# A recurrence on TensorE: part of the second output half's products moved ahead of the wait for the state's second half, its sums in banks by step, its input sums in nine pieces

## The chip, the core and the metric

One core of one Trainium2 chip. The metric is the device time of one execution in microseconds (us), the median of several runs. Engines are named PE (TensorE), ACT (ScalarE), DVE (VectorE), POOL (GpSimd) and SP (the queue that issues most DMAs).

## The reference, cut to what matters

The input x is 8 sequences of 512 steps with 256 features. It passes a recurrence, a long convolution, a gated scan and a mixture of 16 experts. The change is in the recurrence alone:

```python
xw = jnp.einsum('ntd,dh->nth', x, Wx) + b
def step(prev_h, xw_t):
    next_h = jnp.tanh(xw_t + prev_h @ Wh)
    return (next_h, next_h)
_, hs = jax.lax.scan(step, h0, jnp.swapaxes(xw, 0, 1))
```

There are 512 steps, each a product of an 8 x 256 state with a 256 x 256 matrix in float32 and a tanh, and each needs the one before.

## The kernel before

**Layout.** The state is kept transposed: 256 features in two halves of 128 partitions, `k` = 0 and 1 as input and `o` = 0 and 1 as output (h0 and h1 below), with 8 columns, one per sequence. `hring` holds the states of the last 16 steps; it is a part of the tile `tok`, and the trace names it so. PE's 128 columns are used as four tiles of 32 columns (`J` = 4, index `j`), so that one output half is four matmuls per input half. A matmul in float32 stands as two records in the trace, so the 16 matmuls of a step (2 output halves, 2 input halves, 4 tiles) are 32 records of line 531.

**One step** (`steps` on PE, line 523). PE waits for h0 of the step before (`s_h[0]`), multiplies it for o=0, waits for h1 (`s_h[1]`, line 529), multiplies it for o=0 and tells ACT (`s_sum[0]`, line 533). Then it does o=1 on both halves and tells ACT again (`s_sum[1]`). ACT (line 875) waits for each sum and writes tanh of it into `hring`, raising `s_h[0]` and `s_h[1]`.

**Input sums.** The sums of x with Wx and the bias are made eight steps at a time, a *group*, into PSUM, and the state products are added onto them. `inputs_summed(bank, n)` (line 502, matmuls on line 510) does one unit: n runs over the output half and, within it, the bias (`brow`, one row, with a row of ones) and the two halves of x (`xst`). That is six units of 4 matmuls, 64 columns (8 steps x 8 sequences) each. Group 0 of an iteration sums in PSUM banks 0 and 1 (o=0 and o=1), group 1 in banks 2 and 3; while one group's steps run, the other's input sums are made, one unit behind each of the steps t=1 to t=6.

**Filler.** `keep_up(256)` (line 489) is a matmul of zeros into an unused bank. It ends every step except the four (n=11 to 14 of 16) that carry two matmuls each of another part, `kernel_sums` (line 496), which makes the convolution's kernel.

**The other engines in the same loop** of 32 iterations of 16 steps: POOL copies each finished group of states away (line 426) and ACT waits for that once per group. ACT does one exponential for the convolution's kernel (line 879) in four steps. DVE takes the kernel sums out (line 1147), once per iteration. SP loads the x of each group (`ahead`, line 309) when PE has raised `s_xdone` at the group's last input unit; PE waits for the load (`s_xs`) at t=2. Everything behind the loop waits by semaphores for what it needs.

## Time and profile before

| | us |
|---|---|
| median of 3 runs | 1030.88 |
| lowest and highest run | 1028.31, 1051.01 |
| the profiled execution | 1021.49 |
| its span, first to last instruction | 1019.6 |
| PE busy, of the span | 967.6 |
| the recurrence's loop, about | 6.5 to 392 |

The numbers of a row come from the one profiled execution, so sums are made against 1021.49. PE's busy time counts a matmul from its start to its modelled end, and matmuls overlap. "PEld" is the loading of weights, which overlaps the matmuls as well. In a timeline, records of one line are merged into a row with its start, the time from the first start to the last end, and the number of records; `[0.37 <-PE ps L531]` says that the engine was idle for 0.37 us before and what ended it. The PEclk row gives the granted clock in tenths of 2.4 GHz.

### The profile page before, as it was taken

The page shows a single profiled execution, that of the slowest core. Times are in us where ns is not written, and L with a number is a line of the kernel's source. Part 1 is how long each engine was busy: PE and PEld are TensorE (multiplying, and loading weights), DVE is VectorE, ACT ScalarE, POOL GpSimd, SP SyncE. Part 2 cuts the span into 40 slices and gives each one's busy share as a digit, 9 for nine tenths or more (in the row PEclk, how much of TensorE's full clock was granted, in tenths as well). Part 3 has the DMA queues.
Part 4 walks back from the last instruction along what each step waited for, and adds up shares of the span by engine and source line. Part 5 has one row for each costly group of instructions (what it writes and reads, how often), then busy time and mean ns, then how long its engine had stood idle before and what let it go on. Part 6 is the DMA issues. An engine that isn't in the chain of part 4 may idle for free.

```text
span 1019.6 us, 58437 instructions
## 1 busy us (share of the span) xinstructions
PE 967.6 (95%) x25496; PEld 769.3 (75%) x25496; DVE 437.3 (43%) x932; ACT 574.5 (56%) x1956; POOL 309.5 (30%) x308
## 2 busy tenths in 40 slices
PE   8999999999999998779899999899999999999994
PEld 5777777777777777668544444688889999999994
DVE  1000000100000004558489979977556464656550
ACT  3555555555555557659487677623446565656551
POOL 3111111211111111324000346374024545454555
PEclk6999999999999999779899999999999999999998
DMA  3222222244554400875100111054066666566634
GB/s 91 83 93 86 94 100 83 83 78 55 56 60 56 55 11 11 171 141 102 45 0 1 42 42 70 11 207 155 21 204 133 152 130 155 126 155 124 138 43 51
DMA packets 85346, 89.59 MB, mean 88 GB/s; under 512 B 8657, under 2 KB 71654, under 8 KB 85298
## 3 DMA queue, kind: packets, MB, share of 16 engines
q1 hardware_dynamic: 69410, 71.50, 28.0%
q0 software_dynamic: 14592, 17.10, 10.1%
q8 instruction: 29, 0.48, 0.2%
q10 hardware_dynamic: 1296, 0.37, 0.2%
q14 instruction: 19, 0.16, 0.1%
HBM read 56.82 MB, written 33.96 MB: 89 GB/s over the span
## 4 chain that ended last, share of the span: by engine, by line
PE 80%; issue 5%; DVE 4%; POOL 4%; ACT 3%; DMA 3%; ACTq 0%; POOLq 0%; SPq 0%; DVEq 0%
PE ps L531 21%; PE ps L806 15%; PE ps L489 8%; PE ps L820 8%; PE ps L672 8%; PE ps L510 7%; PE ps L722 3%; POOL slots_in L452 2%; PE ps L594 2%; PE ps L579 2%; PE ps L496 2%; PE ps L731 2%; DMA slots_in<-tok,arena 1%; PE ps L582 1%; PE ps L749 1%
## 5 line engine op out<-in xcount | busy, mean ns | idle before, releaser
L875 ACT ACTIVATE tok<-ps 128x8 f32<-128x8 f32 x1024 | 172.8, 178 | 184.8 <-PE ps L531 184.2
L531 PE MATMUL ps<-tok,wh 128*32 128x8 f32 x16384 | 250.4, 181 | 2.3 <-ACT tok L875 2.1
L531 PEld LDWEIGHTS ps<-tok,wh 128*32 128x32 f32 x16384 | 203.4, 112 | 62.3 <-ACT tok L875 11.8
L1147 DVE TENSOR_SCALAR arena<-ps 128x127 f32<-128x127 f32 x32 | 9.3, 290 | 348.0 <-PE ps L496 348.0
L471 POOL DMA_INDIRECT out<-arena,dest x80 | 127.9, 1598 | 98.9 <-ACT arena L1033 79.7
L806 PE MATMUL ps<-xgT_hi,ew_hi 128*128 128x320 f32 (+1 forms) x384 | 118.8, 309 | 3.7 <-DVE spare L1288 1.6
L806 PE MATMUL ps<-xgT_hi,ew_lo 128*128 128x320 f32 (+1 forms) x384 | 119.0, 310 | 0.0
L806 PE MATMUL ps<-xgT_lo,ew_hi 128*128 128x320 f32 (+1 forms) x384 | 118.2, 308 | 0.0
L489 PE MATMUL ps<-zero 128*128 128x256 bf16 (+1 forms) x392 | 113.6, 293 | 1.3 <-POOL zero L399 1.3
L1394 DVE TENSOR_TENSOR mid<-mid,ps 128x320 f32<-128x320 f32 (+1 forms) x96 | 46.6, 486 | 106.0 <-issue 52.4
L672 PE MATMUL ps<-mid,gw 128*128 128x512 f32 x192 | 85.6, 604 | 2.4 <-ACT mid L961 1.6
L510 PE MATMUL ps<-xst,wx 128*32 128x64 f32 x2080 | 83.0, 227 | 0.0
L1051 ACT ACTIVATE mid<-ps 128x320 f32<-128x320 f32 (+1 forms) x96 | 41.9, 436 | 72.2 <-PE ps L806 68.8
L426 POOL TENSOR_TENSOR big<-tok,zero 128x128 f32 x64 | 28.9, 451 | 170.8 <-ACT tok L875 170.8
L452 POOL DMA_INDIRECT slots_in<-tok,arena x64 | 73.4, 1147 | 23.6 <-issue 17.1
L404 POOL TENSOR_TENSOR arena<-dta_q,iota_t 128x512 f32<-128x512 f32 x33 | 34.3, 1039 | 149.3 <-PE ps L496 148.2
L672 PEld LDWEIGHTS ps<-mid,gw 128*128 128x128 f32 x192 | 36.8, 194 | 47.7 <-issue 46.4
L806 PEld LDWEIGHTS ps<-xgT_hi,ew_hi 128*128 128x128 f32 (+1 forms) x384 | 68.7, 179 | 4.4 <-DVE spare L1288 1.9
L820 PE MATMUL ps<-ew_hi,eact_hi 128*128 128x256 f32 (+1 forms) x240 | 71.7, 299 | 0.3 <-ACT arena L1033 0.3
L806 PEld LDWEIGHTS ps<-xgT_lo,ew_hi 128*128 128x128 f32 (+1 forms) x384 | 68.8, 179 | 0.0
L806 PEld LDWEIGHTS ps<-xgT_hi,ew_lo 128*128 128x128 f32 (+1 forms) x384 | 68.6, 179 | 0.0
L820 PE MATMUL ps<-ew_hi,eact_lo 128*128 128x256 f32 (+1 forms) x240 | 67.8, 282 | 0.0
(206 smaller groups left out, 1782.5 us busy)
## 6 DMA issues: line engine op xcount, KB each, us to landing
ring<-k_pad SPq DMA_DIRECT2D x64, 256.0 KB, 6.3
slots_in<-mid SPq DMA_DIRECT2D x16, 645.0 KB, 3.5
mid<-slots_in SPq DMA_DIRECT2D x16, 645.0 KB, 4.2
arena<-in_ex_down SPq DMA_DIRECT2D x16, 384.0 KB
arena<-in_ex_gate SPq DMA_DIRECT2D x16, 352.0 KB
arena<-in_ex_up SPq DMA_DIRECT2D x16, 352.0 KB
xst<-in_x_steps SPq DMA_DIRECT2D x66, 64.0 KB, 1.8
xtok<-in_x_tok SPq DMA_DIRECT2D x16, 256.0 KB, 2.8
```

The costliest lines, as they stand in the source:

```text
L404: pool.tensor_tensor(kqx, d.unsqueeze(2).to_broadcast([P, KG * NH, P]), iota_t[:].unsqueeze(1).to_broadcast([P, KG * NH, P]), ALU.mult).th ...
L452: pool.indirect_dma_start(out=slots_in[:, :], out_offset=bass.IndirectOffsetOnAxis(ap=idx[:, k, r:r + 1], axis=0), in_=hid_tok[:, r, :], i ...
L471: pool.indirect_dma_start(out=out[:, :], out_offset=bass.IndirectOffsetOnAxis(ap=dest[:, z, t:t + 1], axis=0), in_=yo[:, z, t], in_offset= ...
L489: nc.tensor.matmul(ps[:, 6, 0:columns], zero16[:, 0:P], zero16[:, 0:columns], start=True, stop=True)
L510: last = nc.tensor.matmul(ps[Q * j:Q * j + Q, 2 * bank + o, 0:G * B], w, v, start=c < 0, stop=c == C - 1, skip_group_check=True, tile_posi ...
L531: last = nc.tensor.matmul(sums_at(bank, t, o)[Q * j:Q * j + Q], wh[:, k, columns(j, o)], hring[:, (n - 1) % (2 * G), k], start=False, stop ...
L672: last = nc.tensor.matmul(ps[:, gate_bank(n % NT, q), :], gw[:, q, c, z * P:(z + 1) * P], x1T[:, c, 4 * b:4 * b + 4, :].rearrange("p r t - ...
L806: last = nc.tensor.matmul(ps[0:fw, 2 * h + m % 2, 0:HALF], of(w)[:, c, f0:f0 + fw], v[:, c, hf * HALF:(hf + 1) * HALF], start=c == 0 and p ...
L820: last = nc.tensor.matmul(ps[:, 4 + (z + t) % 2, 0:D], a[0:fw, f, t * P:(t + 1) * P], down_of(w)[0:fw, f], start=f == 0 and p == 0, stop=f ...
L875: nc.scalar.activation(hring[:, n, o], sums_at(n // G, n % G, o), ACT.Tanh).then_inc(s_h[o], 1)
L1051: nc.scalar.activation(esil[0:fw, m % 2], ps[0:fw, m % 2, 0:HALF], ACT.Silu).then_inc(s_esil, 1)
L1394: nc.vector.tensor_tensor(eprod[0:fw, m % 2], esil[0:fw, m % 2], ps[0:fw, 2 + m % 2, 0:HALF], ALU.mult).then_inc(s_eact, 1)
```

## The change

Four things are changed, all in the recurrence.

1. In each step, the matmuls of the first two column tiles of o=1 on h0 are issued before the wait for h1. Those of the other two tiles come after o=0 is complete.
2. o=0's sums of a group stay in one bank (0 or 1), with even steps in its first half and odd ones in its second. o=1's sums go to a bank by the step's parity: banks 2 and 3 for group 0, 5 and 7 for group 1. The host orders each group's x in the same way (even steps, then odd).
3. The input sums are nine units: three of 64 columns for o=0, and three of 32 columns for each of the two banks of o=1. They stand behind the steps t=1 (two), t=2 (two), t=3, t=4, t=5 (one each) and t=6 (two).
4. `keep_up(256)` is called at t=0 and t=7 alone.

```diff
--- before.py
+++ after.py
@@ -260,7 +260,9 @@
         FIRST_LOADED, STATE_LOADED, LOADED, LATE = 16 * len(first), 16 * len(state), 16 * len(loads), 16 * len(late)
 
         NT = 2 * C
-        NIN = C * (C + 1)
+        LATER = (2, 3, 5, 7)
+        NIN = 3 * (C + 1)
+        INPUTS = {1: (0, 2), 2: (2, 4), 3: (4, 5), 4: (5, 6), 5: (6, 7), 6: (7, NIN)}
 
         def gate_bank(t, q):
             return (2 * t) % 6 + q if q < 2 else 2 + t
@@ -273,7 +275,10 @@
 
         def sums_at(bank, t, o):
 
-            return ps[:, 2 * bank + o, B * t:B * t + B]
+            if o == 0:
+                at = B * (G // 2 * (t % 2) + t // 2)
+                return ps[:, bank, at:at + B]
+            return ps[:, LATER[2 * bank + t % 2], B * (t // 2):B * (t // 2) + B]
 
         def columns(j, o):
 
@@ -501,16 +506,26 @@
 
             def inputs_summed(bank, n):
 
-                o, c = n // (C + 1), n % (C + 1) - 1
+                part, c = n // (C + 1), n % (C + 1) - 1
+                o, at = ((0, slice(0, G)), (1, slice(0, G // 2)), (1, slice(G // 2, G)))[part]
+                to = (bank, LATER[2 * bank], LATER[2 * bank + 1])[part]
+                cols = B * (at.stop - at.start)
                 for j in range(J):
                     if c < 0:
-                        w, v = brow[0:1, columns(j, o)], ones
+                        w, v = brow[0:1, columns(j, o)], ones[:, 0:cols]
                     else:
-                        w, v = wx[:, c, columns(j, o)], xst[:, bank, c].rearrange("p t b -> p (t b)")
-                    last = nc.tensor.matmul(ps[Q * j:Q * j + Q, 2 * bank + o, 0:G * B], w, v, start=c < 0, stop=c == C - 1,
+                        w, v = wx[:, c, columns(j, o)], xst[:, bank, c, at].rearrange("p t b -> p (t b)")
+                    last = nc.tensor.matmul(ps[Q * j:Q * j + Q, to, 0:cols], w, v, start=c < 0, stop=c == C - 1,
                                             skip_group_check=True, tile_position=(0, Q * j))
                 return last
 
+            def state_product(bank, t, o, k, groups):
+
+                n = bank * G + t
+                for j in groups:
+                    last = nc.tensor.matmul(sums_at(bank, t, o)[Q * j:Q * j + Q], wh[:, k, columns(j, o)], hring[:, (n - 1) % (2 * G), k],
+                                            start=False, stop=k == C - 1, skip_group_check=True, tile_position=(0, Q * j))
+                return last
             for _ in range(WARM):
                 keep_up(512)
             pe.wait_ge(s_ps0, 1)
@@ -523,21 +538,20 @@
             def steps(i, bank):
                 for t in range(G):
                     n = bank * G + t
-                    for o in range(C):
-                        for k in range(C):
-                            if o == 0:
-                                pe.wait_ge(s_h[k], 2 * G * i + n + 1)
-                            for j in range(J):
-                                last = nc.tensor.matmul(sums_at(bank, t, o)[Q * j:Q * j + Q], wh[:, k, columns(j, o)], hring[:, (n - 1) % (2 * G), k],
-                                                        start=False, stop=k == C - 1, skip_group_check=True, tile_position=(0, Q * j))
-                        last.then_inc(s_sum[o], 1)
-                    if t == 2:
-                        pe.wait_ge(s_xs[1 - bank], 16 * i + 16 + 16 * bank)
-                    if 1 <= t <= NIN:
-                        last = inputs_summed(1 - bank, t - 1)
-                        if t == NIN:
+                    pe.wait_ge(s_h[0], 2 * G * i + n + 1)
+                    state_product(bank, t, 0, 0, range(J))
+                    state_product(bank, t, 1, 0, range(J // 2))
+                    pe.wait_ge(s_h[1], 2 * G * i + n + 1)
+                    state_product(bank, t, 0, 1, range(J)).then_inc(s_sum[0], 1)
+                    state_product(bank, t, 1, 0, range(J // 2, J))
+                    state_product(bank, t, 1, 1, range(J)).then_inc(s_sum[1], 1)
+                    for u in range(*INPUTS.get(t, (0, 0))):
+                        if u == 1:
+                            pe.wait_ge(s_xs[1 - bank], 16 * i + 16 + 16 * bank)
+                        last = inputs_summed(1 - bank, u)
+                        if u == NIN - 1:
                             last.then_inc(s_xdone, 1)
-                    if not 11 <= n < 11 + 2 * NH:
+                    if t in (0, G - 1):
                         keep_up(256)
                     if 11 <= n < 11 + 2 * NH:
                         if n == 11:
@@ -1458,7 +1472,7 @@
     a_log, c_re, dt = np.asarray(L0_attn_A_log), np.asarray(L0_attn_C_re), np.asarray(L0_attn_log_dt)
     d_k = np.zeros((J, Q, IT), f32)
     d_k[:KG, :J] = np.asarray(L0_attn_D).reshape(J, IT, KG).transpose(2, 0, 1)
-    steps = x.reshape(B, S // G, G, C, P).transpose(1, 4, 3, 2, 0)
+    steps = x.reshape(B, S // G, G // 2, 2, C, P).transpose(1, 5, 4, 3, 2, 0).reshape(S // G, P, C, G, B)
     consts = np.zeros((P, 8), f32)
     consts[np.arange(P), np.arange(P) // Q] = 1
     consts[:, 4] = -(np.arange(P) + 1)
```

How PE's instructions stand is shown at two places. Here tok,wh are a state product, spare,brow a bias product, xst,wx a product with x, and zero the filler. First the step t=1 of the loop's first group, before:

```order
L531 MATMUL ps<-tok,wh 32x8 [waits s_h0]
L531 MATMUL ps<-tok,wh 32x8 x3
L531 MATMUL ps<-tok,wh 32x8 [waits s_h1]
L531 MATMUL ps<-tok,wh 32x8 x11
L510 MATMUL ps<-spare,brow 32x64 x4
L489 MATMUL ps<-zero 128x256
```

The same step on PE after the change:

```order
L526 MATMUL ps<-tok,wh 32x8 [waits s_h0]
L526 MATMUL ps<-tok,wh 32x8 x5
L526 MATMUL ps<-tok,wh 32x8 [waits s_h1]
L526 MATMUL ps<-tok,wh 32x8 x9
L518 MATMUL ps<-spare,brow 32x64 x4
L550 REGISTER_ALU
L518 MATMUL ps<-xst,wx 32x64 [waits s_xs1]
L518 MATMUL ps<-xst,wx 32x64 x3
```

Two state products have moved from behind the wait for h1 to ahead of it, the first product with x stands here with its wait for the load, and the filler is gone. Next the end of step t=2 on PE, before (its state products stand as in t=1):

```order
L535 REGISTER_ALU
L510 MATMUL ps<-xst,wx 32x64 [waits s_xs1]
L510 MATMUL ps<-xst,wx 32x64 x3
L489 MATMUL ps<-zero 128x256
L529 REGISTER_ALU
```

The end of the same step on PE after:

```order
L518 MATMUL ps<-xst,wx 32x64 x4
L518 MATMUL ps<-spare,brow 32x32 x4
L541 REGISTER_ALU
```

A bias unit of 32 columns, o=1's first, has taken the place of the filler.

## Rows read from the trace of the kernel before

**Rows 1.** The page: granted clock by slice, the chain by line, two groups of instructions.
```profile
PEclk6999999999999999779899999999999999999998
...
PE ps L531 21%; PE ps L806 15%; PE ps L489 8%; PE ps L820 8%; PE ps L672 8%; PE ps L510 7%; PE ps L722 3%; POOL slots_in L452 2%; PE ps L594 2%; PE ps L579 2%; PE ps L496 2%; PE ps L731 2%; DMA slots_in<-tok,arena 1%; PE ps L582 1%; PE ps L749 1%
...
L531 PE MATMUL ps<-tok,wh 128*32 128x8 f32 x16384 | 250.4, 181 | 2.3 <-ACT tok L875 2.1
...
L510 PE MATMUL ps<-xst,wx 128*32 128x64 f32 x2080 | 83.0, 227 | 0.0
```

**Rows 2.** Busy time by engine, count, clock, DMA: the recurrence at full clock.
```profile
26.50:392.50 366.00, 365.93 (x19659) 276.97 (x19653) 28.87 (x92) 191.96 (x1115) 57.99 (x92) 1.00 0.33 70
```

**Rows 3.** Who waited for whom, 40 to 380 us: in total, times, longest.
```profile
ACT tok L875 <- PE ps L531: 161.8, 460, 0.5
...
PEld ps L531 <- ACT tok L875: 8.2, 52, 0.2
```

**Rows 4.** Timeline of DVE: start, us, instruction; L1147 in iterations 3 and 16.
```profile
48.54 0.29 DVE L1147 TENSOR_SCALAR arena<-ps 128x127 f32<-128x127 f32 x1 [10.71 <-PE ps L496]
...
202.46 0.29 DVE L1147 TENSOR_SCALAR arena<-ps 128x127 f32<-128x127 f32 x1 [10.71 <-PE ps L496]
```

**Rows 5.** Timeline of PE, steps of one iteration; x counts matmul records.
```profile
67.61 0.53 PE L531 MATMUL ps<-tok,wh 128*32 128x8 f32 x32
68.08 0.31 PE L510 MATMUL ps<-spare,brow 1*32 1x64 f32 x8
68.33 0.28 PE L489 MATMUL ps<-zero 128*128 128x256 bf16 x1
68.54 0.44 PE L531 MATMUL ps<-tok,wh 128*32 128x8 f32 x32
68.81 0.32 PE L510 MATMUL ps<-xst,wx 128*32 128x64 f32 x8
...
71.79 0.28 PE L496 MATMUL ps<-arena 128*4 128x64 f32 x4
```

**Rows 6.** Timeline of ACT in the same stretch: one row for a step's two tanh.
```profile
68.09 0.34 ACT L875 ACTIVATE tok<-ps 128x8 f32<-128x8 f32 x2 [0.37 <-PE ps L531]
68.92 0.34 ACT L875 ACTIVATE tok<-ps 128x8 f32<-128x8 f32 x2 [0.49 <-PE ps L531]
...
70.37 0.34 ACT L875 ACTIVATE tok<-ps 128x8 f32<-128x8 f32 x2 [0.37 <-PE ps L531]
...
72.49 0.34 ACT L875 ACTIVATE tok<-ps 128x8 f32<-128x8 f32 x2 [0.37 <-PE ps L531]
```

**Rows 7.** Timeline of PE at the half clock, in the first nine steps.
```profile
9.22 0.53 PE L531 MATMUL ps<-tok,wh 128*32 128x8 f32 x32 [2.08 <-ACT tok L875]
...
10.38 0.62 PE L531 MATMUL ps<-tok,wh 128*32 128x8 f32 x32
...
11.18 0.39 PE L489 MATMUL ps<-zero 128*128 128x256 bf16 x1
11.51 0.62 PE L531 MATMUL ps<-tok,wh 128*32 128x8 f32 x32
...
16.13 0.62 PE L531 MATMUL ps<-tok,wh 128*32 128x8 f32 x32
...
17.00 0.62 PE L531 MATMUL ps<-tok,wh 128*32 128x8 f32 x32
```

**Rows 8.** Windows again: a stretch in which PE idles, and the next; PEclk is third last.
```profile
422.40:425.80 3.40, 1.29 (x24) 0.79 (x16) 2.20 (x7) 3.40 (x10) 1.95 (x1) 1.00 0.93 206
425.80:429.20 3.40, 2.84 (x64) 2.56 (x68) 0.44 (x2) 0.05 (x1) 0.00 (x0) 0.50 0.94 207
```

**Rows 9.** The page's DMA issues (KB, us to landing), then the timeline of SP and PE.
```profile
xst<-in_x_steps SPq DMA_DIRECT2D x66, 64.0 KB, 1.8
...
263.89 0.38 SPq L309 DMA_DIRECT2D xst<-in_x_steps  x1
...
270.09 0.32 PE L510 MATMUL ps<-xst,wx 128*32 128x64 f32 x8
```

## The prediction

> **What bounds the kernel now.** I read four views in this order. The page first: the clock row is full in nearly every slice, and the chain by line puts L531 at 21%, L489 at 8%, L510 at 7% and L496 at 2% of the span [rows 1]. All four lines stand in the recurrence, which fills the first 392 us. The stage window then shows that in 366 us of it PE counts 365.93 us as busy at the full clock [rows 2]. That figure doesn't say what a step waits for, because a state product has 8 columns and its record is mostly latency. The waits come third: ACT waited for L531 in 460 steps, 161.8 us in all, while PE waited for ACT only 52 times [rows 3]. So in most steps the tanh results were there before PE had worked through its queue.
>
> The timelines say which. ACT's rows show two kinds of step. From 70.37 to 72.49 three steps take 2.12 us, 0.707 each; from 68.09 to 68.92 one takes 0.83 [rows 6]. In the first kind every link waits for the link before it: h1 lands, the four products of o=0 on h1 end, tanh 0 runs, tanh 1 follows on ACT, the next step starts. Its two tanh take 0.34 us together, the second starting 0.16 behind the first, although one is 0.18 long, so the second waits for ACT and not for its sums. In the other kind PE's queue is late: behind the state products stand the input sums (L510) and then the 256-column product with zeros (L489), and only 0.21 us after that one's start do the next state products begin (68.33 to 68.54) [rows 5].
>
> The whole iteration of 16 steps is read from DVE's L1147, once per iteration: 13 iterations from 48.54 to 202.46 are 153.92 us, or 11.84 each [rows 4]. Sixteen waited steps would be 16 x 0.707 = 11.31. Filler on PE therefore costs 0.53 us per iteration, 17 us in 32, and 0.707 a step is the floor of this form of the recurrence.
>
> **The half block between the waits.** Two products of o=1 on h0 move ahead of the wait for h1. Behind that wait stood 4 products of o=0 and then 8 of o=1; now 4 and 6. I give this nothing on the chain: tanh 0 needs the same 4 products after h1, and tanh 1 is held by ACT. Ahead of the wait there is room in a waited step: the 8 records of h0's products and the gap behind them end where h1 arrives. A price arises only where PE comes late, since the half block then stands before the sums that tanh 0 needs. The trace has no pair of 8-column products alone. From below: 4 records at the pace of L531, (0.44 - 0.18) / 31 = 8.5 ns each, are 0.034 us [rows 1, 5]. From above: as much as a whole block of 8 records, 0.068. The nearest rows are two products of 64 columns (L496), whose 4 records spread over 0.28 less some 0.22 = 0.06, against 0.10 for the 8 records of L510 [rows 1, 5]; halving the column tiles halves the time by less than half. I take 0.05, and PE is free 0.01 earlier at the step's end.
>
> **Banks by step.** Other banks for o=1 change no duration that I can name: 0. They force o=1's input sums into two parts of 32 columns, so six units become nine.
>
> **Eight keep-up products removed.** Before, 12 of 16 steps ended with L489; after, 4 (t=0 and t=7 of both groups). All eight that go stood behind input sums. L489 alone, as t=0 and t=7 keep it, starts 0.10 behind the last state product and holds PE for 0.21 more: 0.35 + 0.10 + 0.21 = 0.66 from the step's start, under 0.707. Steps with one unit come to the floor as well: last state product at 0.35, xst's last start 0.11 behind (68.80 to 68.91), and PE is ready at about 0.5.
>
> **The two units of t=1 and t=2, from a step's first product.** A waited step's records span 0.53 and one is 0.18 long [rows 1, 5], so the last starts at 0.35. With the 0.01 taken off, 0.34 to 0.35. For t=1 the bias row follows 0.11 later (67.96 to 68.08), its last starts 0.09 on (0.31 less L510's 0.22), and the next shape 0.15 behind that (68.18 to 68.33) [rows 1, 5]: xst starts at 0.70. Its second half starts 0.08 later (my estimate from the spread of 0.10) and 64 columns take 0.05, the gap between L496's pairs. Next state products: 0.83. From there to tanh 0 an unwaited step takes 68.92 - 68.54 = 0.38 [rows 5, 6]; plus 0.05 for the half block, minus 0.02 since no start-up gap stands in a full queue: 1.24. The chain wants tanh 0 at 0.48 (67.61 to 68.09) + 0.707 = 1.19. Late: 0.06 with the uncut numbers. For t=2, xst follows directly (last start 0.46), the bias row of 32 columns after a change of shape at 0.61, its spread 0.07, a change back 0.12 (between 0.10 behind 8 columns and 0.15 behind 64): 0.80, tanh 0 at 0.80 + 0.38 + 0.05 = 1.23. Late: 0.05.
>
> On a switch of tile shape the trace shows 0.10 to 0.15 us without a start; the Trainium skill ("TensorEngine Tiling (Array Packing)", Key Properties) says that changing the tiling mode drains the engine, and the trace agrees. The same page (Instruction Overhead) says that a matmul with one column has the latency of one with 60; by it the 32-column pieces cost what 64 columns cost, and t=2 would be late by another 0.03 or so; no run here shows 32 columns yet, and L531's 8 columns run at 8.5 ns a record, quicker than that rule allows.
>
> Elsewhere: t=6 has two xst units of 32 columns, no switch, 0.13 at most; t=5 one bias piece, with only one change of shape on either side. Both end before the floor.
>
> **Sum.** 0.53 - 2 x (0.06 + 0.05) = 0.31 us per iteration. It counts for 31 iterations (the first ran at the half clock): 9.6 us. At the half clock, steps took 1.13 with xst (10.38 to 11.51) and 0.87 with L489 alone (16.13 to 17.00), and L489 there costs 0.33 (11.18 to 11.51) [rows 7]. Six of them out of eight steps are 2.0 us, of which I give back 1.0 for the doubled units; over some 14 steps, at what a step costs later, that is 1.3 us, an estimate. Together 10.9. The three more pieces of the first input sums lie ahead of a PE wait of 2.08 us for ACT (9.22) [rows 7]: nothing.
>
> **Other engines.** xst is now wanted one step earlier and a group sooner over. The tightest transfer I found is issued at 263.89 and used at 270.09; landing takes 1.8 (median), so some 4 us were spare and 3 stay [rows 9]. ACT is idle 0.37 of 0.707 between its pairs [rows 6]; the exponentials in four of the steps go into that. What comes after the recurrence waits by semaphores and moves up as a whole. Its low-clock stretches may fall differently, some 3 us either way.
>
> The profiled execution took 1021.49 us (span 1019.6), 9.4 below the runs' median of 1030.88. Its own time would be 1010.6; the median 1030.88 - 10.9 = 1020.0.
>
> **Rivals.**
> *The half block is cheap.* If it costs 0.02 to 0.03 in a full queue and the switches overlap, t=1 and t=2 are late by 0.04 together: 0.45 x 31 + 1.3 = 15 us, time 1016; with the clock rising a stretch or two earlier, up to 20, time 1011. For it: only 4 records; against it: L496's spread.
> *The clock falls (the slower side).* With 8 of 12 keep-ups gone PE may be granted 1.2 GHz in the recurrence. Place: t=3 to t=5, where least is left. [...] Against it: at full clock it fell to half where PE had been busy 1.29 us of 3.40 (422.4, then 425.8) [rows 8], and the new steps leave it busy over 90%. Price: a step at half clock costs at least 0.87, not 0.72, 0.15 each: all of it, 495 x 0.15 = 74 us, time 1094. It cancels the gain from 11 / 0.15 = 73 such steps on, and is slower by over 2% from about 210. The Trainium skill ("TensorE: Matmul & The Clock Gate", The HAM clock gate) says that the throttled state is the default and activity lifts it; it would price this alike.
> *The switches eat it.* If a 32-column piece costs as much as 64 and each drain is 0.03 dearer, t=1 and t=2 are late by 0.20 together: 0.13 x 31 + 1 = 5 us, time 1026.
> *Nothing.* Filler was hidden anyway: 1031. Against it, the step of 0.83.
>
> **How the numbers follow.** Forecast 0.50, cheap half block 0.20, switches 0.17, clock 0.07, nothing 0.06. Range: 1010 (half block free, early clock) to 1030 (switches, and a worse fall of later clock stretches); it leaves the clock case and thin tails out. Over 2% is 20.6 us, about what a measurement of this kernel tells from no change: faster 0.11 from the cheap case's tail, slower 0.07 from the clock case.
>
> **What would show it.** Right: ACT's pairs 0.707 apart in steps t=3 to t=7 and t=0, about 0.77 behind t=1 and t=2; the iteration 11.5 by L1147; the clock row unchanged from 26 us on. The half block's cost shows in the first start of o=0's products on h1 behind t=1. Wrong: a half clock past 30 us, a step below 0.70, or PE waiting for xst's transfer.

## The result, and the profile after the change

The changed kernel takes 1003.66 us (median of 4 runs, 998.22 to 1014.48) against 1029.6 us for the kernel before, measured beside it (4 runs). The ratio is 0.9746, with a 95% interval of 0.970 to 0.9793. Here and below, a ratio and its interval leave out executions over 1.5% above the fastest of the same kernel, which the medians keep. Some 26 us were saved where 10.9 had been forecast, and the time lies below the forecast range of 1010 to 1030.

Against itself: the profiled execution took 1004.57 us (span 1002.7), that of before 1021.49 (span 1019.6). These 16.9 us are what the two traces can explain.

The page of the kernel after: the clock row, the chain by line, and the two groups of PE that answer to [rows 1].

```profile
PEclk6589999999999999899899999999999999999997
...
PE ps L526 21%; PE ps L820 17%; PE ps L518 9%; PE ps L834 8%; PE ps L686 8%; PE ps L494 3%; PE ps L736 3%; POOL slots_in L457 3%; PE ps L501 2%; PE ps L745 2%; PE ps L593 2%; ACT tok L889 2%; PE ps L608 1%; DMA slots_in<-tok,arena 1%; PE ps L763 1%
...
L526 PE MATMUL ps<-tok,wh 128*32 128x8 f32 x16384 | 259.2, 182 | 13.5 <-issue 3.0
...
L518 PE MATMUL ps<-xst,wx 128*32 128x64 f32 (+1 forms) x3120 | 106.7, 212 | 0.0
```

L526 is the state product (L531 before), L518 the input sums (L510), L494 the product with zeros (L489), whose share of the chain falls from 8% to 3%. The second and third slices of the clock row are the surprise: PE stays at the half clock longer than before. The two windows of the recurrence, with PEclk third last, bound it (against [rows 2]):

```profile
8.30:56.00 47.70, 43.83 (x1988) 36.24 (x1992) 2.21 (x9) 17.12 (x107) 9.05 (x10) 0.50 0.19 68
56.00:380.00 324.00, 315.63 (x19626) 255.55 (x19619) 27.91 (x89) 164.26 (x1045) 55.53 (x88) 1.00 0.35 72
```

DVE's L1161 (L1147 before) stands once in each iteration and answers to [rows 4]. Its timeline:

```profile
78.41 0.29 DVE L1161 TENSOR_SCALAR arena<-ps 128x127 f32<-128x127 f32 x1 [10.15 <-PE ps L501]
89.57 0.29 DVE L1161 TENSOR_SCALAR arena<-ps 128x127 f32<-128x127 f32 x1 [10.03 <-PE ps L501]
```

That is 11.16 us an iteration instead of 11.84. The timelines of PE (first fence) and of ACT (second) over the steps of t=1 and t=2 answer to [rows 5, 6]:

```profile
118.58 0.50 PE L526 MATMUL ps<-tok,wh 128*32 128x8 f32 x32
119.01 0.31 PE L518 MATMUL ps<-spare,brow 1*32 1x64 f32 x8
119.25 0.32 PE L518 MATMUL ps<-xst,wx 128*32 128x64 f32 x8
119.39 0.43 PE L526 MATMUL ps<-tok,wh 128*32 128x8 f32 x30
...
119.68 0.30 PE L518 MATMUL ps<-xst,wx 128*32 128x64 f32 x6
119.91 0.26 PE L518 MATMUL ps<-spare,brow 1*32 1x32 f32 x8
120.10 0.43 PE L526 MATMUL ps<-tok,wh 128*32 128x8 f32 x30
```

```profile
118.35 0.30 ACT L889 ACTIVATE tok<-ps 128x8 f32<-128x8 f32 x2 [0.37 <-PE ps L526]
119.02 0.30 ACT L889 ACTIVATE tok<-ps 128x8 f32<-128x8 f32 x2 [0.37 <-PE ps L526]
119.80 0.30 ACT L889 ACTIVATE tok<-ps 128x8 f32<-128x8 f32 x2 [0.48 <-PE ps L526]
120.55 0.30 ACT L889 ACTIVATE tok<-ps 128x8 f32<-128x8 f32 x2 [0.44 <-PE ps L526]
121.22 0.30 ACT L889 ACTIVATE tok<-ps 128x8 f32<-128x8 f32 x2 [0.37 <-PE ps L526]
```

Read ACT's rows as in [rows 6]. A waited step is now 0.67 (118.35 to 119.02), not 0.707, and the pair of tanh is 0.30 long, not 0.34. The idle time between pairs stayed 0.37; the step lost what the pair lost (the gap between the two starts went from 0.159 to 0.126, the step from 0.706 to 0.671). The steps behind t=1 and t=2 take 0.78 and 0.75.

The 16.9 us split so, by the differences of all tanh starts, step by step. At the full clock an iteration has eleven steps of 0.67, steps of 0.787 and 0.742 behind t=1 and t=2 of either group, and one of 0.712 with kernel sums (behind n=13): 11.157 against 11.84, and 29 iterations times 0.683 save 19.8. The first three iterations took 18.84, 14.73 and 14.51 us, where before took 16.59, 12.09 and 11.84: 7.6 lost. Of these, 5.3 lie in the second and third, which ran at the half clock here and, but for 0.9 us, at the full clock before. The other 2.25 lie in the first, which ran at the half clock in both kernels, and the clock does not explain them. There four steps took 1.85, 2.11, 1.91 and 1.78 (behind n=5, 9, 11 and 14), and PE waited for nothing that the profile shows. Its waits in the window 9 to 28, of this kernel and of before (us in all, times, longest):

```profile
PE ps L526 <- issue: 3.0, 4, 0.9
```

```profile
PE ps L531 <- issue: 0.2, 1, 0.2
```

In the later iterations at the half clock these steps take 0.83, 1.15, 0.81 and 0.85, some 4.0 us less. So PE stalled only the first time it went through the loop. What follows the recurrence took 622.8 instead of 627.4: 4.6 saved (the clock was at half for 17.1 us of it, in before for 27.3). Together 16.8.

### The profile page after: what moved, and what is told of

Read it like the earlier page. It is cut to its first block, busy times and chain, and to the rows that moved or that the text cites. A ratio compares the mean times of both kernels' runs of the same rounds, so it can differ in the third digit from the quotient of the medians.

```text
span 1002.7 us, 61045 instructions
## 1 busy us (share of the span) xinstructions
PE 938.8 (94%) x26800; PEld 768.1 (77%) x26800; DVE 437.5 (44%) x932; ACT 556.7 (56%) x1956; POOL 314.4 (31%) x308
## 4 chain that ended last, share of the span: by engine, by line
PE 77%; issue 5%; ACT 5%; DVE 4%; POOL 4%; DMA 2%; ACTq 0%; POOLq 0%; DVEq 0%
PE ps L526 21%; PE ps L820 17%; PE ps L518 9%; PE ps L834 8%; PE ps L686 8%; PE ps L494 3%; PE ps L736 3%; POOL slots_in L457 3%; PE ps L501 2%; PE ps L745 2%; PE ps L593 2%; ACT tok L889 2%; PE ps L608 1%; DMA slots_in<-tok,arena 1%; PE ps L763 1%
## 5 line engine op out<-in xcount | busy, mean ns | idle before, releaser
L526 PE MATMUL ps<-tok,wh 128*32 128x8 f32 x16384 | 259.2, 182 | 13.5 <-issue 3.0
L526 PEld LDWEIGHTS ps<-tok,wh 128*32 128x32 f32 x16384 | 216.1, 115 | 61.2 <-ACT tok L889 25.6
L889 ACT ACTIVATE tok<-ps 128x8 f32<-128x8 f32 x1024 | 155.3, 177 | 190.1 <-PE ps L526 190.0
L1161 DVE TENSOR_SCALAR arena<-ps 128x127 f32<-128x127 f32 x32 | 9.3, 290 | 335.9 <-PE ps L501 335.9
L518 PE MATMUL ps<-xst,wx 128*32 128x64 f32 (+1 forms) x3120 | 106.7, 212 | 0.0
L457 POOL DMA_INDIRECT slots_in<-tok,arena x64 | 76.3, 1192 | 23.6 <-issue 17.1
L518 PEld LDWEIGHTS ps<-xst,wx 128*32 128x32 f32 x3120 | 69.4, 114 | 6.5 <-issue 1.0
```

The lines of the kernel that those rows point to most:

```text
L457: pool.indirect_dma_start(out=slots_in[:, :], out_offset=bass.IndirectOffsetOnAxis(ap=idx[:, k, r:r + 1], axis=0), in_=hid_tok[:, r, :], i ...
L518: last = nc.tensor.matmul(ps[Q * j:Q * j + Q, to, 0:cols], w, v, start=c < 0, stop=c == C - 1, skip_group_check=True, tile_position=(0, Q ...
L526: last = nc.tensor.matmul(sums_at(bank, t, o)[Q * j:Q * j + Q], wh[:, k, columns(j, o)], hring[:, (n - 1) % (2 * G), k], start=False, stop ...
L889: nc.scalar.activation(hring[:, n, o], sums_at(n // G, n % G, o), ACT.Tanh).then_inc(s_h[o], 1)
```

## The experiments

All times of groups are medians of device time, with the ratio to the kernel before, measured beside them, and its 95% interval. "Step" is the distance between two first tanh, "gap" that between the first and the second tanh of a step. A "waited" step is one in which PE waits for the tanh and not the tanh for a late PE. "Clock full from" is the end of the half clock at the start.

**Order or banks?** Two theories for the 0.034 that the waited step lost. The order: with two products of o=1 ahead of the wait for h1, only 6 instead of 8 stand between the end of o=0's sums and the end of o=1's, so the second tanh starts earlier. The banks: o=1's sums now change bank with each step, so what reads and what writes no longer meet. Three kernels separate them. The first keeps the banks and pieces, with nothing ahead:

```diff
                     state_product(bank, t, 0, 0, range(J))
-                    state_product(bank, t, 1, 0, range(J // 2))
                     pe.wait_ge(s_h[1], 2 * G * i + n + 1)
                     state_product(bank, t, 0, 1, range(J)).then_inc(s_sum[0], 1)
-                    state_product(bank, t, 1, 0, range(J // 2, J))
+                    state_product(bank, t, 1, 0, range(J))
```

> The changed kernel with all of o=1's products behind the wait for h1, as before; banks by step, nine pieces and four keep-ups stay. Theory A (the second tanh starts when o=1's sums are done, so each product behind the wait is on the chain): the two tanh are 0.159 us apart again, a waited step takes 0.707, an iteration 11.6 to 11.7, and the time is about 14 us above the changed kernel's. Theory B (the banks let ACT start its second tanh earlier; the order does nothing): 0.126 apart, 0.671, an iteration about 11.15, no change.

Measured: 1016.72 us, ratio 0.9859 (0.9799 to 0.9919). Waited step 0.7045, gap 0.159, as before; iteration 11.50; clock full from 55.7 us. ACT's timeline at 300 us:

```profile
300.17 0.34 ACT L888 ACTIVATE tok<-ps 128x8 f32<-128x8 f32 x2 [0.16 <-PE ps L526]
...
300.87 0.34 ACT L888 ACTIVATE tok<-ps 128x8 f32<-128x8 f32 x2 [0.17 <-PE ps L526]
```

The pair is 0.34 long again and the step 0.70 (the idle time is only 0.16 here because one of the exponentials stands between, in the row left out). The banks alone give the waited step nothing.

The second is the kernel before, with only its filler taken out:

```diff
-                    if not 11 <= n < 11 + 2 * NH:
+                    if t in (0, G - 1):
                         keep_up(256)
```

> The kernel before with the keep-up products at t=0 and t=7 alone; order, banks and six pieces as before. Both theories: the two tanh 0.159 us apart, a step 0.707 to 0.716, an iteration 11.32 to 11.40, which is 0.44 to 0.52 less than before, some 14 to 16 us in all at full clock. If the clock rises later, as in the profile of the changed kernel, up to 7 us of that are lost at the start; if the late rise came by chance, it rises at about 26 us.

Measured: 1009.7 us, ratio 0.9822 (0.9774 to 0.987). Every step 0.704 to 0.705, gap 0.159, iteration 11.27. So the filler cost 11.84 - 11.27 = 0.57 us per iteration (0.53 in the forecast). That is most of what the change gains: order, banks and pieces together take only 11.27 - 11.157 = 0.11 more off an iteration, 3 us in 29, and the intervals of the two ratios overlap. Ten waited steps give 0.33 and the step behind n=15 0.03; the steps behind t=1, t=2 and n=13 take back 0.25.

The kernel above has an iteration 0.23 longer than this one. Of this, 0.12 stands behind t=1 and t=2 (0.753 and 0.717 against 0.704), the price of the two pieces a step without the half block, where 0.22 had been forecast with it. The other 0.11 is one step, the last of the iteration, 0.812 against 0.704. That step differs between kernels whose steps are otherwise the same (0.676 in the changed kernel, see also the filler ahead of the loop below); why isn't known. The clock rose at 55.3 us here, although order and pieces are those of before. So fewer keep-up products alone went with the late rise.

The third puts all four products on h0 ahead:

```diff
-                    state_product(bank, t, 1, 0, range(J // 2))
+                    state_product(bank, t, 1, 0, range(J))
                     pe.wait_ge(s_h[1], 2 * G * i + n + 1)
                     state_product(bank, t, 0, 1, range(J)).then_inc(s_sum[0], 1)
-                    state_product(bank, t, 1, 0, range(J // 2, J))
```

> The changed kernel with all four products of o=1 on h0 ahead of the wait. Theory A: the two tanh come closer than 0.126 (0.09 to 0.10), but 16 records then stand ahead of the products that tanh 0 needs, which start 0.15 to 0.16 after the step's first, so a step takes 0.67 to 0.70, no gain on the changed kernel. Theory B: 0.126 apart, 0.671 to 0.70.

Measured: 1007.87 us, ratio 0.9809 (0.9762 to 0.9856). Iteration 11.075, gap 0.093, waited step 0.678, clock full from 55.5 us. ACT's timeline at 300 us:

```profile
300.28 0.27 ACT L888 ACTIVATE tok<-ps 128x8 f32<-128x8 f32 x2 [0.41 <-PE ps L526]
300.96 0.27 ACT L888 ACTIVATE tok<-ps 128x8 f32<-128x8 f32 x2 [0.41 <-PE ps L526]
```

The pair shrinks again, to 0.27, but the idle time before it grows from 0.37 to 0.41: four products ahead of the wait are more than the room there, so tanh 0 comes later by what tanh 1 gains, and a little more.

The gap follows the count. With 8, 6 and 4 products between the two ends it is 0.159, 0.126 and 0.093: 0.0165 us for each product, which is two records at 8.3 ns. The order is shown as the cause, the banks are not.

**Pieces one a step.** The two units of t=1 and t=2 with their changes of tile shape are spread:

```diff
-        INPUTS = {1: (0, 2), 2: (2, 4), 3: (4, 5), 4: (5, 6), 5: (6, 7), 6: (7, NIN)}
+        INPUTS = {1: (0, 1), 2: (1, 3), 3: (3, 4), 4: (4, 6), 5: (6, 7), 6: (7, NIN)}
```

> The changed kernel with the nine pieces placed so that no step has a change of tile shape between two of its units: t=1 the bias of 64 columns, t=2 two of x with 64, t=3 a bias of 32, t=4 two of x, t=5 a bias, t=6 two of x. If the 0.115 and 0.072 us by which t=1 and t=2 exceed 0.671 come from two changes of shape in one step, both go: an iteration of 10.8 to 10.9 for 11.16, 8 to 12 us less in all. If they come from the amount of work, t=2 stays above 0.72 and the gain is under 6 us.

Measured: 999.56 us (997.64 to 1001.49), ratio 0.9716 (0.9672 to 0.976). The steps behind t=1 and t=2 are 0.675 and 0.672, the iteration 10.89. So the late steps behind t=1 and t=2 cost 0.36 us per iteration. The iteration is only 11.157 - 10.89 = 0.27 shorter, since the steps behind n=11 and n=15 became longer by 0.09. In 29 iterations 0.27 is 7.8 us, as expected; the medians show 4.1. In its profiled execution this kernel's clock rose only at 68.9 us, one more iteration at the half clock (14.1 against 10.9, so 3 us).

**Does more filler bring the clock up sooner?** The half clock at the start had grown from 17 us to 48. The first kernel keeps all keep-up products in the first two iterations, which are written out for that:

```diff
-                    if t in (0, G - 1):
+                    if t in (0, G - 1) or (type(i) is int and not 11 <= n < 11 + 2 * NH):
                         keep_up(256)
...
-            with pe.Fori(0, IT) as i:
+            for i in range(2):
+                for bank in range(2):
+                    steps(i, bank)
+            with pe.Fori(2, IT) as i:
```

> The changed kernel, whose first two iterations alone have the keep-up product in every step without kernel sums, as before. If the missing keep-ups made the clock rise at 56 us and not at 26, it rises at 20 to 30 us here, and the time is 4 to 8 us under the changed kernel's. If the late rise was chance or comes from the new order or the pieces, it stays at 56 us and the time is the same or up to 3 us more.

Measured: 1060.36 us, ratio 1.0334 (1.0275 to 1.0393), slower than the kernel before, and neither expectation held: half clock to 111.4 us, and what follows the recurrence took 655.9 instead of 622.8. From its waits, on PE's weight loads (us in all, times, longest):

```profile
PEld ps L596 <- issue: 22.6, 13, 10.7
...
PEld ps L611 <- issue: 20.9, 14, 5.4
```

L596 and L611 stand behind the recurrence and are not part of the edit. PE waited there for nothing that the profile shows, up to 10.7 us at once. In the changed kernel the same two lines waited 7.0 and 7.4 us, so 29 of the 33 us are these waits. The second iteration, written out as well, stalls like the first (steps of up to 2.28). The experiment is spoilt by its own means, since writing out two passes changed the time elsewhere. It can't tell what the filler did.

The next two put 10 products of 512 columns with zeros behind step 0, written out for one iteration only; the second of them has the spread pieces too.

```diff
                         keep_up(256)
+                    if type(i) is int and n == 0:
+                        for _ in range(10):
+                            keep_up(512)
...
-            with pe.Fori(0, IT) as i:
+            for i in range(1):
+                for bank in range(2):
+                    steps(i, bank)
+            with pe.Fori(1, IT) as i:
```

> The changed kernel with ten keep-up products of 512 columns between the first step and the second, where PE now waits about 2 us for ACT's first tanh and the clock falls. If that idle stretch makes the clock fall, it stays full from about 5 us on, no step of the recurrence runs at half, and the time is 10 to 14 us under the changed kernel's. If the light work of the steps makes it fall, the clock is half again by 12 us, with a gain under 3 us.

> The pieces placed as in the run with no change of shape inside a step, and the ten keep-up products of 512 columns between the first two steps. If both gains hold and add: an iteration of 10.9, full clock throughout the recurrence, 984 to 989 us. If the clock falls without the filler of t=1 and t=2, some 995.

Measured: 1031.77 us, ratio 0.992 (0.9874 to 0.9965), and 1022.2, ratio 0.9914 (0.9876 to 0.9953). The clock was full until 15.5 and 16.6 us, then half until 90.6 and 132.7. It did not fall when the filler ended. PE's timeline of the first of the two:

```profile
7.45 2.44 PE L494 MATMUL ps<-zero 128*128 128x256 bf16 x10
9.82 0.46 PE L526 MATMUL ps<-tok,wh 128*32 128x8 f32 x32
...
14.33 0.32 PE L526 MATMUL ps<-tok,wh 128*32 128x8 f32 x17 [0.71 <-issue]
```

The row of L494 merges the 256-column product of step 0 with the 512-column ones behind it and names the first. The filler ends at 9.9, and the steps behind it run at the full clock, 0.67 each. Then PE stalls, as in every first iteration but that of before, and the clock has fallen 1.2 us later. It came back later, not sooner. Whether the stall made it fall isn't shown.

With no pass written out, the same ten products ahead of the loop:

```diff
+            for _ in range(10):
+                keep_up(512)
             with pe.Fori(0, IT) as i:
```

> The changed kernel with ten products of 512 columns ahead of the loop, which PE does while ACT isn't ready for the first tanh; nothing is written out twice. If unrolling (instructions that run once and are waited for) cost what the two unrolled runs lost, the time is within 1% of the changed kernel's, and 3 to 10 us under it if the clock also stays full through the first iteration. If the bridge itself does harm, it is 1010 us or more.

Measured: 1021.88 us (13 runs, 1010.8 to 1055.67), ratio 0.9903 (0.9867 to 0.9938). Half clock from 15.2 to 202.9 us in the profiled execution, again with a stall of PE just before the fall (1.01 us, until 14.11). That execution took 1049.73 and is one of the five longest; the eight of 1010.8 to 1023.84 have a mean granted clock of 0.940 to 0.968, against 0.895 in it, so their half clock was shorter. This is worse than without, once more, but not by the clock alone. The loop is that of the changed kernel, yet the last step of each iteration takes 0.90 at the full clock, not 0.676, and the iteration 11.39. ACT's timeline around that step, here and in the changed kernel:

```profile
294.40 0.30 ACT L891 ACTIVATE tok<-ps 128x8 f32<-128x8 f32 x2 [0.37 <-PE ps L526]
295.30 0.30 ACT L891 ACTIVATE tok<-ps 128x8 f32<-128x8 f32 x2 [0.60 <-PE ps L526]
```

```profile
257.16 0.30 ACT L889 ACTIVATE tok<-ps 128x8 f32<-128x8 f32 x2 [0.37 <-PE ps L526]
257.83 0.30 ACT L889 ACTIVATE tok<-ps 128x8 f32<-128x8 f32 x2 [0.37 <-PE ps L526]
```

And the changed kernel with the keep-up products back in 12 of 16 steps:

```diff
-                    if t in (0, G - 1):
+                    if not 11 <= n < 11 + 2 * NH:
                         keep_up(256)
```

> The changed kernel with the keep-up product in all twelve steps that had it before; order, banks and nine pieces as changed. Theory: PE's queue is late again and hides what the order gains on the chain. Steps with two units and the filler take 0.85 to 0.95, steps with one 0.70 to 0.74, an iteration 11.7 to 12.1, and the time is that of the kernel before within 1%. The clock rises at about 26 us. If instead the order alone carried the gain, an iteration is under 11.4.

Measured: 1077.94 us, ratio 1.0495 (1.0419 to 1.0571). Iteration 12.7, above the 11.7 to 12.1 expected, and the time 5% above that of before, where within 1% was expected; the step behind t=1 is 1.140. PE's timeline shows three things in a row behind the state products, each of another tile shape:

```profile
297.23 0.50 PE L526 MATMUL ps<-tok,wh 128*32 128x8 f32 x32
297.66 0.31 PE L518 MATMUL ps<-spare,brow 1*32 1x64 f32 x8
297.91 0.32 PE L518 MATMUL ps<-xst,wx 128*32 128x64 f32 x8
298.16 0.28 PE L494 MATMUL ps<-zero 128*128 128x256 bf16 x1
298.37 0.40 PE L526 MATMUL ps<-tok,wh 128*32 128x8 f32 x26
```

The next state products start 1.14 behind the first, of which 0.25 lie between the bias row and xst, 0.25 between xst and the zeros, and 0.21 to the state products. The half clock lasted to 132.3 us, where a rise at about 26 was expected, so the filler was no cover against it either. Nine pieces are affordable only with the filler gone: the two edits belong together.

**Even load.** The spread pieces, with two more changes: the four kernel sums moved to n=8, 12, 14 and 15, and keep-up left at n=0 and n=7 alone (two of 16 steps instead of four):

```diff
+            SUMS_AT = (8, 12, 14, 15)
...
-                    if t in (0, G - 1):
+                    if n in (0, G - 1):
                         keep_up(256)
-                    if 11 <= n < 11 + 2 * NH:
-                        if n == 11:
+                    if n in SUMS_AT:
+                        if n == SUMS_AT[0]:
...
-                        kernel_sums(n - 11)
+                        kernel_sums(SUMS_AT.index(n))
```

> The pieces placed without a change of shape inside a step, and the convolution kernel's four sums moved from the steps 11 to 14 to the steps 8, 12, 14 and 15, away from the bias pieces (keep-up products at n=0 and n=7 alone). The steps n=11 and n=13, 0.711 us there, go to 0.672; n=15 stays at 0.67 to 0.72. An iteration of 10.75 to 10.85 for 10.89, so 1 to 4 us less than that kernel's 999.6, if ACT's exponentials and POOL's arguments for the next iteration still come in time; if they don't, a step of 0.8 or more appears at n=2 or n=8.

Measured: 1075.3 us (6 runs, 1072.49 to 1082.32), ratio 1.047 (1.0422 to 1.0518). Steps 0.807 to 0.93 through the whole recurrence, iteration 13.6. The clock row and the group of the state product on its page, and a window of it:

```profile
PEclk9999999999999999999989999999999999999997
...
L526 PE MATMUL ps<-tok,wh 128*32 128x8 f32 x16384 | 329.1, 205 | 5.5 <-issue 3.8
```

```profile
200.00:300.00 100.00, 100.00 (x4972) 85.97 (x4963) 7.09 (x24) 41.40 (x264) 13.88 (x22) 1.00 0.33 60
```

The row says full clock, but the records do not: the mean of L526 is 205 ns, where the other kernels have 179 to 181 in stretches with the full clock (200 to 300 us) and 203 to 206 in stretches with the half (15 to 25 us). The waited step is 0.807, the value that every changed kernel here has at the half clock. So the recurrence ran at the half clock throughout, in a trace that shows no change of clock before the recurrence's end and so takes it as full. The other executions bear it out: two of them, at 1073.3 and 1074.83 us, have a mean granted clock of 0.782 and 0.781, against 0.988 in the profiled one of 1075.78. A share of 0.22 missing is 467 us at half, the recurrence (440 us) and a little more. That is the slower rival of the prediction: 75.7 us above the kernel with spread pieces, where 74 had been priced. The expected 10.75 to 10.85 was missed by far, and which of the two added changes did it was not tried.

**Three ahead.** The spread pieces, and three of the four products ahead of the wait:

```diff
-                    state_product(bank, t, 1, 0, range(J // 2))
+                    state_product(bank, t, 1, 0, range(3))
...
-                    state_product(bank, t, 1, 0, range(J // 2, J))
+                    state_product(bank, t, 1, 0, range(3, J))
```

> The pieces placed without a change of shape inside a step, and three of the four products of o=1 on h0 ahead of the wait. Theory A: two products fewer between the sums than with one ahead... in numbers 10 records between o=0's and o=1's end, so the two tanh are 0.109 us apart (0.159, 0.126 and 0.093 were measured with none, two and four ahead). The chain alone would give a step of 0.655; the products ahead of the wait fill the time until h1 comes, so 0.655 to 0.675, and the time within 4 us of 999.6.

Measured: 994.31 us (6 runs, 989.11 to 1009.88), ratio 0.9681 (0.9624 to 0.9737), the lowest median of all kernels, though its interval overlaps that of the spread pieces alone. Gap 0.109, waited step 0.672, iteration 10.82. The first change of clock in its trace is the rise at 41.2 us; before it the row says full, but the records of L526 are 204 ns long and the steps 0.81 and more. Of the 5.3 us under the spread pieces, two fewer iterations at the half clock can account for more than all. ACT's timeline at 300 us:

```profile
300.87 0.29 ACT L889 ACTIVATE tok<-ps 128x8 f32<-128x8 f32 x2 [0.38 <-PE ps L526]
301.54 0.29 ACT L889 ACTIVATE tok<-ps 128x8 f32<-128x8 f32 x2 [0.39 <-PE ps L526]
```

The pair is 0.29 and the wait before it 0.38. The third product shortens the pair by 0.017 and delays tanh 0 by as much: of the counts tried, the waited step is shortest with two or three ahead. What the iteration gains (0.07) comes mainly from three steps, two behind kernel sums (n=11 and 13) and the last of the iteration, 0.695 each against 0.711, 0.712 and 0.725.

**The changed kernel once more**, unaltered, to see how much is the single execution.

> The changed kernel once more, unaltered. An iteration of 11.16 at full clock and two tanh 0.126 us apart, as in its first profile. If the moment at which the clock rises is a matter of the single execution, it is not 56 us again and the runs spread over some 15 us; if it is fixed by the kernel, it is 56 us within 3.4. The ratio to the kernel before lies between 0.970 and 0.979.

Measured: 1011.41 us (6 runs, 1000.33 to 1036.08), ratio 0.9779 (0.9716 to 0.9842). In its profiled execution (1010.16 us) the iteration is 11.16 and the gap 0.126, as in the first, but the half clock lasted to about 85 us instead of 56.0. ACT's timeline 60 us into the span, of this execution and of the first:

```profile
60.99 0.30 ACT L889 ACTIVATE tok<-ps 128x8 f32<-128x8 f32 x2 [0.31 <-PE ps L526]
...
61.79 0.30 ACT L889 ACTIVATE tok<-ps 128x8 f32<-128x8 f32 x2 [0.30 <-PE ps L526]
```

```profile
61.76 0.30 ACT L889 ACTIVATE tok<-ps 128x8 f32<-128x8 f32 x2 [0.37 <-PE ps L526]
62.43 0.30 ACT L889 ACTIVATE tok<-ps 128x8 f32<-128x8 f32 x2 [0.37 <-PE ps L526]
```

The same program takes 0.80 a step in the one and 0.67 in the other. Each iteration at the half clock costs 14.7 - 11.16 = 3.5 us, so two more of them are 7 us, and the last tanh starts 7.0 us later here. Between these two executions it is this; for the others, up to 1036.08, there is no trace.

## Why the prediction was wrong

**The step that failed** is in the paragraph on the half block: "I give this nothing on the chain: tanh 0 needs the same 4 products after h1, and tanh 1 is held by ACT." The second half is false. It rested on a comparison: the second tanh starts 0.16 behind the first, one is 0.18 long, so it must wait for ACT. But ACT does not need 0.18 before it starts the next. The trace of before had the row that says so, one I didn't look for, at the program's start, where both sums are ready at once (timeline of ACT in the kernel before):

```profile
8.99 0.24 ACT L875 ACTIVATE tok<-ps 128x8 f32<-128x8 f32 x2
```

0.24 long for two of 0.18 (the starts differ by 0.07), against 0.34 in the recurrence. So tanh 1 waited for its sums, and the eight products between the two ends set the gap. Two fewer take 0.033 off it, h1 lands 0.033 earlier, and the next step's products of o=0 on h1 wait for h1: the whole waited step shrinks by it. The kernels with 0, 2, 3 and 4 ahead show it (0.159, 0.126, 0.109, 0.093). In the ten waited steps it is 0.33 us per iteration, 10 us in 29, before the late steps take a part back; I had it at zero. The kernel with none ahead has an iteration 11.50 - 11.157 = 0.34 longer, but that agrees partly by luck: 0.14 of it is the last step of its iteration, whose length no order explains, and 0.13 goes the other way behind t=1, t=2 and n=13.

**The other steps, in order.**
- The floor of 0.707: right for the kernel before (0.7045 in two others with its order), wrong as a bound that the change could not go under. The forecast's sign of being wrong, a step below 0.70, came true, and so did a half clock past 30 us.
- Banks, nothing: right.
- Filler, 0.53 per iteration: 0.57.
- Half block, 0.05 where PE is late: too dear. In the step t=2, which finds PE's queue full, tanh 0 starts 0.384 behind the step's first product with none ahead, 0.417 with two and 0.450 with four. So the half block costs 0.033, the forecast's lower bound, and the whole block 0.066. The steps behind t=1 and t=2 are 1.53 together (0.786 + 0.743), as the forecast's two times 0.77 are.
- The two units of t=1 and t=2: from the step's first product (118.58), xst starts at 0.67 (forecast 0.70), the next state products at 0.81 (0.83) and tanh 0 at 1.22 (1.24). For t=2 (from 119.39) the bias row starts at 0.52 (0.61), the next products at 0.71 (0.80), tanh 0 at 1.16 (1.23). The change of shape itself was sized right, 0.15 between xst's last start (119.68 + 0.30 less 0.22) and the bias row. The 0.09 were lost before it: I let the state products of t=2 spread over 0.35 as in a waited step, but with a full queue they spread over 0.28. Lateness is larger than forecast nonetheless, 0.115 and 0.072 against 0.06 and 0.05, since the chain had become quicker.
- 32 columns against 64: [rows 5] have the bias row of 64 columns at 0.31 first start to last end, here the one of 32 takes 0.26; ends are modelled, but the eight starts alone spread over 0.10 and 0.08. The Trainium skill ("TensorEngine Tiling (Array Packing)", Instruction Overhead) gives a matmul of one column the latency of one with 60, by which the two should be about equal. The measurement decides, and in this place fewer columns are quicker.
- A gain of 1.3 at the half clock: right step by step, overrun by two things that had no term. Step by step, the changed kernel's second iteration, without stalls, takes 14.7 at the half clock, where before took 16.59 in its first. But the half clock lasted 30 us longer (5.3 lost), and the first iteration had PE's four stalls, which left it 2.25 above before's. The latter is no matter of the clock row. At the half clock the waited step is 0.807 in the old order and the new alike, so there the order gains nothing either; what sets 0.807 I haven't settled.
- xst's transfer, other engines: nothing showed; PE waited for no transfer in the recurrence.
- What follows the recurrence, which was to move up as a whole: it took 4.6 us less than that, a little over the 3 us either way that had been allowed for its stretches at the low clock. They were 10 us shorter.

In numbers: forecast 10.9; plus 0.373 x 29 = 10.8 for the quicker iteration (0.683 for 0.31), minus 2 x 0.31 = 0.6 for two iterations at half clock that I had counted as full, minus 7.6 + 1.3 = 8.9, plus 4.6 behind the recurrence, is 16.8. The rest of the way to 26 us lies in the spread: the profiled execution of before was 8 us under its median. The spread also makes the place against the range a matter of luck. The same kernel's second measurement, 1011.41 us, lies just inside 1010 to 1030; the iteration of 11.16, where 11.5 was forecast, is the same in both.

**The rivals.** "The half block is cheap" had its term right (0.033 for 0.02 to 0.03) and named the right side, but the two late steps did not shrink with it; the gain came from the waited steps, of which it says nothing. "The clock falls" happened in full in the kernel with moved kernel sums, and in the changed kernel in part: it comes up late, at 56 or 85 us. "The switches eat it" and "nothing" fell.

**What stays open:** what decides when the clock rises. It rose at 26.5 us in the kernel before and between 41.2 and 85.1 in all with four of 16 and nothing added, but later still with keep-ups put back or filler added. Two things go together in these traces and were not parted: before is also the only kernel whose first iteration has no stall of PE. What the stalls are is open as well. The rise differs between two executions of one program by 29 us. One version at the half clock throughout, with six runs within 10 us, says that there is an edge nearby; on which side of it a kernel lies I could not foretell. Why the stretches at the half clock behind the recurrence fell shorter was not tried either.

## What to carry to other kernels

When a short instruction starts sooner behind its predecessor than that one is long, the engine overlaps them: the distance of two starts is no proof that the engine holds the second. Look for a place in the trace where both inputs are ready, and compare; here the error that this row would have shown was worth 10 us. In a recurrence split in halves, count the instructions between the ends of the two halves' sums: each counts in full, in every waited step, until those moved ahead of the wait make the first half late. Compare small changes at one clock, not by the median, when the clock's rise alone moves the time by 7 us. And compare step by step, not by the loop's period alone: here the last step of the loop took 0.68 in one kernel and 0.90 in another with the same loop.

## What the runs showed of the hardware that was not expected

- Consecutive state products of 8 columns end 0.0165 us apart (two records each), down to a gap of 0.093 between the two tanh; ACT itself starts two of 0.18 us as little as 0.07 apart.
- PE can be busy in 43.83 of 47.70 us and stay at the half clock. The Trainium skill ("TensorE: Matmul & The Clock Gate", The HAM clock gate) has activity lift it; the window above shows that the busy time of a profile doesn't tell when it will.
- The granted clock in a trace is as good as its first event: three traces (the kernel with moved kernel sums, the one with three ahead, and the changed kernel's second) say 1.00 from the start, while steps of 0.80 and records 0.20 us long say half. In the first of the three, other executions of the same time say 0.78.
- Written-out passes of a loop were dear beyond themselves: with two of them, weight loads much later in the program waited up to 10.7 us with no releaser, and what follows the recurrence took 33 us longer; with one, 11 us longer (633.8 against 622.8).
- PE can stall in the first pass of a loop and in no later one: four times, 3.0 us in all, in the changed kernel, 0.2 us in the kernel before.
- The step across the end of a loop isn't fixed by what stands in it: 0.676 and 0.90 at the full clock in two kernels with the same loop, 0.812 in one with another order.
